# Where a gated feed-forward empties, two of its rounds stand in front of each of the next stage's first two filling rounds

## What is computed

```python
def _layer(x, wqkv, qs, ksc, wo, lg, lb, w1, b1, w2, b2):   # twice
    h = shift_token(x)
    q, k, v = split(h @ wqkv, 3)              # 8 heads of 64
    q, k = l2norm(q) * qs, l2norm(k) * ksc
    q, k = rotary_xpos(q, k)
    x = x + local_attention(q, k, v) @ wo
    h = layer_norm(shift_token(x)) * lg + lb
    a, g = split(h @ w1 + b1, 2)              # 341 wide each
    return x + (a * gelu(g)) @ w2 + b2

def _L1_attn_ref(x, ...):                     # 16 heads of 64
    q = rope(x @ wq.T); latent = x @ w_kv_down.T
    k, v = rope(latent @ w_k_up.T), latent @ w_v_up.T
    return softmax(q k.T / 8 + causal) v @ wo.T
```

## Time and profile before

| | us |
|---|---|
| median of 3 runs | 1570.79 (1569.4 to 1571.27) |
| the profiled execution | 1569.8 |
| its span, first to last instruction | 1568.0 |
| PE, DVE, POOL, ACT busy | 1256.6, 1120.7, 883.2, 734.9 |

### The profile page before, as it was taken

The page is one execution under the profiler, slowest core; times in us unless marked ns, Lnnn a source line. Parts: engine busy times, 40 slices in busy tenths (PEclk is TensorE's granted clock), DMA queues, the critical chain, the costliest instruction groups (busy, mean ns, idle before and its releaser), DMA issues.

```text
span 1568.0 us, 41351 instructions
## 1 busy us (share of the span) xinstructions
PE 1256.6 (80%) x15361; PEld 853.4 (54%) x15361; DVE 1120.7 (71%) x2495; ACT 734.9 (47%) x1529; POOL 883.2 (56%) x1106
## 2 busy tenths in 40 slices
PE   7988878988788878579997888775888885898871
PEld 4556645556545556456665455662555554565540
DVE  6986858984579948558884675434878854898775
ACT  3543435554445544144544453333555542455545
POOL 3543448982379946347663562564566633466654
PEclk9999979998889979889998998886999987999995
DMA  9400000000000000000000000115000012000000
GB/s 332 139 1 1 0 0 0 0 1 23 0 1 0 0 13 2 1 7 1 0 0 1 1 0 28 33 46 175 0 1 1 0 35 64 1 0 2 0 1 27
DMA packets 32472, 36.87 MB, mean 24 GB/s; under 512 B 4451, under 2 KB 29283, under 8 KB 31626
## 3 DMA queue, kind: packets, MB, share of 16 engines
q1 hardware_dynamic: 30410, 32.14, 6.2%
q0 software_dynamic: 1984, 3.67, 0.9%
HBM read 26.63 MB, written 9.18 MB: 23 GB/s over the span
## 4 chain that ended last, share of the span: by engine, by line
PE 38%; DVE 24%; POOL 14%; issue 13%; ACT 7%; DMA 2%; POOLq 1%; DVEq 0%; SPq 0%; ACTq 0%
PE ps L339 31%; DVE maxima L436 6%; PE ps L459 4%; DVE arena L438 4%; POOL inv_norm L909 3%; ACT arena L446 3%; DVE heads_out L769 3%; POOL arena L914 2%; POOL arena L531 2%; PE ps L829 2%; DVE sq_sum L1048 1%; ACT arena L1005 1%; ACT arena L1239 1%; DVE gate L1815 1%; POOL rstd L377 1%
## 5 line engine op out<-in xcount | busy, mean ns | idle before, releaser
L339 PE MATMUL ps<-arena 64*64 64x64 f32 (+5 forms) x7921 | 359.8, 281 | 23.8 <-ACT arena L453 8.3
L339 PEld LDWEIGHTS ps<-arena 64*64 64x64 f32 (+4 forms) x7921 | 218.9, 134 | 156.8 <-issue 125.6
L531 POOL TENSOR_TENSOR arena<-arena,w_const 128x1024 f32<-128x1024 f32 x96 | 182.4, 1901 | 156.5 <-DVE arena L759 69.1
L446 ACT ACTIVATE arena<-arena 128x1024 f32<-128x1024 f32 (+1 forms) x144 | 138.5, 962 | 149.1 <-DVE arena L438 148.8
L436 DVE TENSOR_REDUCE maxima<-ps 128x16 f32<-128x1024 f32 (+1 forms) x144 | 158.7, 1102 | 63.5 <-PE ps L339 61.3
L459 PE MATMUL ps<-w_const,arena 128*128 128x128 f32 x1024 | 143.3, 282 | 41.0 <-ACT arena L446 33.8
L438 DVE TENSOR_TENSOR arena<-ps,maxima 128x1024 f32<-128x1024 f32 (+1 forms) x144 | 159.3, 1106 | 4.9
L377 POOL TENSOR_TENSOR rstd<-var_eps,minus_half 128x1 f32<-128x1 f32 x144 | 80.3, 569 | 131.3 <-DVE var_eps L878 88.9
L909 POOL TENSOR_TENSOR inv_norm<-sq_floor,minus_half 128x16 f32<-128x16 f32 x32 | 122.0, 3812 | 46.9 <-DVE sq_floor L1051 46.6
L459 PEld LDWEIGHTS ps<-w_const,arena 128*128 128x128 f32 x1024 | 115.7, 144 | 58.0 <-ACT arena L446 44.0
L453 ACT COPY arena<-ps 128x1024 f32<-128x1024 f32 (+1 forms) x144 | 131.2, 911 | 19.0 <-PE ps L459 18.5
(11 more groups left out here) (323 smaller groups left out, 2639.1 us busy)
## 6 DMA issues: line engine op xcount, KB each, us to landing
experts<-in_pack_moe SPq DMA_DIRECT2D x2, 4628.0 KB, 21.4
moe_back<-shT SPq DMA_DIRECT2D x4, 1024.0 KB, 20.3
w_fa<-in_pack_fa SPq DMA_DIRECT2D x2, 1024.0 KB, 11.6
moe_in<-state SPq DMA_DIRECT2D x2, 1024.0 KB, 5.0
arena<-moe_back SPq DMA_DIRECT2D x8, 256.0 KB, 5.0
arena<-moe_back SPq DMA_DIRECT2D x4, 512.0 KB, 5.1
w_a<-in_pack_a SPq DMA_DIRECT2D x1, 1856.0 KB, 18.0
w_fg<-in_pack_fg SPq DMA_DIRECT2D x2, 537.0 KB, 12.4
```

The costliest lines, as they stand in the source:

```text
L339: return nc.tensor.matmul(o, lhsT, rhs, start=start, stop=stop, skip_group_check=True)
L446: nc.scalar.activation(probs(s)[:, 0:n], probs(s)[:, 0:n], ACT.Exp, scale=scale)\
L531: nc.gpsimd.tensor_tensor(keys_wide(s).rearrange("p (b h t) -> p b h t", b=SEQS, h=8), key8(s).rearrange("p (b t) -> p b t", b=SEQS).unsqu ...
```

## The change

Behind a feed-forward stage (`last_ph in GLU`: F0_GLU and F1_GLU) the four emptying rounds are no longer put one before each of the next stage's four filling rounds. Two stand before its first filling round and two before its second; the third and fourth have none before them. It is the same on all four engines, since all use this function. All other seams keep their order, and no instruction is added or removed.

```diff
             for ph, depth, step in parts + [(None, 0, None)]:
                 back = -(-max(depth, last_depth) // 2)
+                ahead = last_ph in GLU
                 for j in range(back):
                     for n in STREAMS:
-                        if last_step:
+                        if last_step and ahead and j == 0:
+                            for m in STREAMS:
+                                last_step(tiles_at(whole(last_ph, TURNS + n), m))
+                        elif last_step and not ahead:
                             last_step(tiles_at(whole(last_ph, TURNS + j), n))
                         if step:
                             step(tiles_at(whole(ph, j), n))
```

## The result

The changed kernel took 1555.86 us (1550.26 to 1557.17) against 1570.1 for the kernel before in the same comparison: a ratio of **0.9903** (95% interval 0.9877 to 0.9929), 14.2 us less. Repeated twice it gave 0.9888 (0.9872 to 0.9904) and 0.9905 (0.9889 to 0.9922). The forecast was 1557.7 us, 13.1 less. The profiled execution took 1556.3 us with a span of 1554.5, so 13.5 us less span than before.

What follows compares the result with a forecast made beforehand. It took order-made holes at two seams, not a busy engine, as what the change could win. Gains of 4.8 and 8.3 us sum to 13.1, taking the median from 1570.8 to 1557.7 us; range 1550.5 to 1565.5.

Steps and rivals of the forecast that it cites:

- The mechanism: Both seams: PE and POOL holes come from instruction order alone; late filling rounds lose waits, the first two inherit some.
- First seam, cost: F0_GLU to F1_ATTN: the first two tiles each start about 2 us late.
- First seam, gain: F0_GLU to F1_ATTN: 4.8 us gained, between 3.8 and 5.9 by the ruler, bounds 2 to 7.6.
- the ruler of F0_ATTN: Same code filling with nothing in front: norms(0) to softmax(1) takes 27.9 us there, 36.0 in F1_ATTN before.
- Second seam, cost: F1_GLU to L1_ATTN: turn_x(0) 3.1 us late, and tile 1, from stage(1), 6.2 us late.
- Second seam, gain: F1_GLU to L1_ATTN: rotate_queries(3) 12.3 us earlier at full clock, taken as 8.3 with a mixed clock.
- a lump for the clock: Second seam: 4.0 us taken off for slow matmuls, of 10.6 if all on the path ran at half clock.
- The signs: Expected trace marks: gated(15) ahead of unit(0), PE hole some 5 us, rotate_queries(3) 7 to 12 us early, steady periods unchanged.
- everything at half clock: Both seams' fills at half clock throughout: gain 3.7 us, 1567.1 us; chance 0.08.
- Full clock throughout: Both seams, PE granted full clock nearly throughout: gain 19.9 us, 1550.9 us; chance 0.11.
- That the holes only move: Both seams: the waits go but as much comes back ahead of the first two filling rounds, 1570.8 us; chance 0.05.
- The slower case: Both seams: lateness of first tiles carried through, 1579.2 us, deciding if rotate_queries(2) starts later than 671.3; chance 0.05.

Runs made afterwards that it cites:

- only_e17: Kernel before with only the second emptying round moved, ahead of the first filling round, at both seams; ratio to before 0.9987.
- only_e18_e19: Kernel before with the second, third and fourth emptying rounds all ahead of the second filling round, first filling round left on time; ratios to before 0.9906, repeated 0.9893.
- e19_later: Kernel before with the second and third emptying rounds ahead of the second filling round, the fourth ahead of the third; ratio to before 0.9943.
- after3: The changed kernel run again, unaltered, as neighbour of other variants on the same chip; ratio to before 0.9905.
- hoist_keep: Changed kernel with POOL's stage(1) ahead of the third emptying round, plus 15 and 22 filler matmuls in PE's holes; 1547.4 us, ratio to before 0.9857.
- seam1: Kernel before with the new order only behind F0_GLU, the second seam keeping the old order; ratio to before 0.9990.
- hoist: Changed kernel with POOL's stage(1) of L1_ATTN put ahead of the third emptying round, not behind norm_pool(15); ratio to before 0.9884.
- after2: The changed kernel run again, unaltered, beside other variants on the same chip; ratio to before 0.9888.
- all_first: Kernel before with all four emptying rounds ahead of the first filling round; ratio to before 0.9909.
- keep: Changed kernel with 10 filler matmuls at the first seam and 14 at the second, in PE's hole ahead of the third emptying round; ratio to before 0.9890.

## Why the prediction was right, step by step

**The mechanism** held. The holes came from order, and E18 and E19 ahead of N2 and N3 were all of it that can be measured (only_e17, only_e18_e19). At the second seam it was above all E19, whose norm_pool(15) stood ahead of stage(3): with it left ahead of N2, e19_later keeps 2.7 of the 8.7 us there.

**The sum** was 13.1 us; the span fell by 13.5. Of these the two seams are 11.9, and 1.6 came in stretches where the prediction had nothing. What lies outside the seams also differs by up to 6 us between kernels on one chip whose work there is the same (1468.4 us in after3, 1462.1 in hoist_keep), so 1.6 is within what such traces differ by, and that the sum came out within 0.4 is luck.

**First seam, cost: right.** norms(0) came 4.8 us behind down(13) before and 7.1 after: 2.2 late, as worked out. project(1) is 2.8 late instead of 2.0, with down(15) at half clock (1.62); in the traces with 0.91 it is 2.0.

**First seam, gain: 3.2 in this trace, 4.0 in three others, for 4.8.** norms(0) to softmax(1) took 30.6 us; the ruler of F0_ATTN said 27.9 to 30.0. The ruler was good, and the middle of it too kind: project(1) took 3.61 us, so the slow end, 3.8, was the right reading. It left out the wait of 4.52 us for POOL, which was 0.23 us at the start of F0_ATTN. The walk at full speed, 7.6, is out of reach: even hoist_keep gains 5.6 there.

**Second seam, cost: 3.1 was right, 6.2 was short.** turn_x(0) is 3.0 late. stage(1) is 8.4 late (21.3 behind down(13) against 13.0). I had the slow clock begin in the hole from 644; it began at project_queries(0), 3.56 us instead of 1.98, and down(15) took 1.62 instead of the 0.9 of the walk. These two make up the missing 2.2 us.

**Second seam, gain: 8.7 for 8.3.** The walk at full clock gave 12.3, and 4.0 were taken off as a lump for the clock, a choice between 0 and 10.6. What came off is 3.6. It all came off early: tile 1 is late by 8.0 us and not 4.2, and rotate_queries(2) therefore only 0.9 early and not 4.8. From there to rotate_queries(3) it took 11.0 us at a granted clock of 1.00, as in the walk (11.3). So the lump had the right size, and tiles 0 and 1 should have carried it. That it fits within 0.4 us is luck: held against the old order in seam1's trace, which had the slower clock, the same new seam gains 12.1. A filler wins 2.1 us of the lump back (hoist to hoist_keep), with one projection still slow.

**The signs.** As forecast: the order of gated(15) and unit(0), the hole of some 5 us on PE (4.92), rotate_queries(3) 7 to 12 us early, the steady periods. Not as forecast: softmax(1) 30.6 us behind norms(0) and not 27.9 to 30; stage(1) 8.4 late for 6; rotate_queries(2) 0.9 early for 5.

**The rule of the Trainium skill** ("TensorE: Matmul & The Clock Gate", section "HAM oscillation — how this bites in real kernels"), that the burst behind a wait starts cold, agrees with this case in part. down(15) of the second seam took 1.62 us behind a wait of 4.92 us, and 0.83 us in hoist_keep, where a filler stood in that wait. But at the first seam, behind the same 3.44 us, it took 1.62 us in two traces (the changed kernel's first, hoist) and 0.91 in three (after2, after3, seam1), and project_queries(0) ran at half clock behind a wait of 0.35 us, where it had run at full clock behind the same wait before. As a case of its own (everything at half clock, 1567.1) it didn't come true: the mean granted clock over the second seam was 0.82 after and 0.79 before. The window of the changed kernel from down(13) to rotate_queries(3):

```profile
629.00:677.72 48.72, 31.25 (x270) 19.41 (x274) 25.88 (x46) 11.80 (x22) 19.97 (x18) 0.82 0.02 6
```

The clock got better with the new order and not worse, as the idle time on PE shrank (22.8 to 17.5 us).

**The cases.** Full clock throughout (19.9 us less in the seams) is what hoist_keep comes near, with 17.6, but with a filler and stage(1) moved; the order alone doesn't reach it. That the holes only move: at the first seam they largely did, 3.4 and 4.5 us in place of the 7.9 for gated(14) and gated(15), and the gain there is in shorter waits elsewhere and in the clock. At the second seam 4.9 and 2.2 us replace 13.9 (for gated(14), gated(15) and stage(3)), and the case fails. The slower case priced the lateness of tiles 0 and 1 in full. It fell with all_first and only_e18_e19: tile 0 between 5.8 and 15.7 us behind down(13) leaves the second seam at 48.7. Its point of decision, rotate_queries(2), was close, 0.9 us from the other side, but it decided little: the gain came behind it, from stage(3).

## What to carry to other kernels

Where two pipelines meet on engines that work in order, ask for each round of the old stage which engine it makes wait and what stands behind that engine. What paid here was to put the last rounds of the old stage ahead of the second tile of the new one, all together: the first tile could be late for nothing at the second seam (6.7 us more of it cost nothing), and nearly so at the first (3.9 us more cost about 1), while one leftover norm ahead of the third tile cost 6 us. Measure such a seam within each trace, between two events that every variant has, and look at its granted clock before comparing: here the clock moved one seam by 3.4 us, with the same work in it.

## What the runs showed of the hardware

With 10 and 14 filler matmuls the larger matmuls behind them still ran at half clock, and the kernel was no faster. With 15 and 22 of them, and the other hole closed as well, those ran at full clock, and the two seams were 4.6 us shorter than in hoist, in one trace of each. The clock also differs from one execution to the next: the same matmuls, down(15) at the first seam, took 1.62 or 0.91 us behind the same wait of 3.44 us. And the mean granted clock of a seam doesn't tell its length: keep had 0.93 over its second seam and hoist 0.82, and they took 47.6 and 47.5 us. The filler's own fast matmuls count in that mean, and nobody waits for them.
